# A vision block on one Trainium2 core: two of four adding tiles loaded whole and halved by GpSimd, the causal mask added by TensorE, the second variance moved to GpSimd

## What is computed

```python
def tok(x, channel_weights):                  # 14x14 patches of 16x16
    pooled = x.reshape(64, 12, 14, 16, 14, 16).sum(axis=(3, 5))
    return einsum('bcij,ce->bije', pooled, channel_weights).reshape(64, 196, 192)

def attn(x, ...):                             # 12 heads of 16
    q, k_, v = split(x @ Wqkv_w + Wqkv_b)
    scores = einsum('bthd,bshd->bhts', q, k_ / sqrt(16))
    scores = scores + triu(full(-10000.0), 1)              # causal mask
    attn_output = (softmax(scores) @ v) @ out_w + out_b
    selection = softmax((x @ sel_w + sel_b) / temperature)[..., 1:]
    idx = top_k(selection[..., 0], 14)                     # 14 of 196 tokens
    return x.at[idx].add((attn_output * selection)[idx])

def ffn(x, ...):
    return gelu(x @ in_weight.T + in_bias) @ out_weight    # 192 -> 768 -> 192

h = tok(x)
h = h + attn(layernorm(h))
h = h + ffn(layernorm(h))
```

## Time and profile before

| | |
|---|---|
| median of 3 runs | 710.67 us (710.17 to 711.61) |
| the profiled execution | 711.4 us, of which 709.7 us span |
| busy share of the span: TensorE, DVE, ScalarE, GpSimd | 82%, 75%, 48%, 22% |
| mean granted TensorE clock | 0.935 of 2.4 GHz |
| HBM read, written | 159.0 MB, 12.7 MB |
| mask adds of groups 0 and 15 start at | 108.1 and 671.4 us |

### The profile page before, as it was taken

One profiled execution on the slowest core, in us unless ns is written; L12 is line 12 of the kernel. 1 busy time (PEld: TensorE's weight loads), 2 busy tenths in 40 slices (PEclk: granted clock), 3 DMA queues, 4 the chain that ended last, 5 costly groups with the idle time before them and its releaser, 6 DMA issues.

```text
span 709.7 us, 12208 instructions
## 1 busy us (share of the span) xinstructions
PE 583.1 (82%) x3860; PEld 469.5 (66%) x3860; DVE 533.0 (75%) x1357; ACT 342.9 (48%) x826; POOL 156.6 (22%) x212
## 2 busy tenths in 40 slices
PE   0237268989997998989988959989998999899995
PEld 0126146667966786768776847768776877778774
DVE  0695968798979798888978865888989897855411
ACT  0000236565656556565656435565656474647451
POOL 1021312131232223222322203222322223102001
PEclk9967557999999999999999979999999999999999
DMA  9997998999999999999999998899999997501011
GB/s 315 298 330 221 289 308 201 304 270 316 259 315 267 317 253 313 286 296 277 282 316 251 286 231 248 229 304 241 305 308 278 280 282 214 109 9 37 4 35 40
DMA packets 66382, 172.56 MB, mean 243 GB/s; under 512 B 4457, under 2 KB 56873, under 8 KB 60171
## 3 DMA queue, kind: packets, MB, share of 16 engines
q1 hardware_dynamic: 32512, 110.11, 44.3%
q0 software_dynamic: 26112, 44.73, 35.5%
q10 hardware_dynamic: 7690, 16.89, 7.1%
...
## 4 chain that ended last, share of the span: by engine, by line
PE 32%; DVE 27%; DMA 18%; issue 13%; ACT 5%; POOL 2%; ACTq 2%; POOLq 0%; DVEq 0%
PE psO L590 9%; DVE R L888 8%; DMA X<-in_x 6%; DMA patch_sums<-R 5%; DMA OB<-in_ob 5%; PE psS L529 3%; PE psS L541 3%; PE psF L578 2%; PE psC L565 2%; DVE a_ln L898 2%; DVE y_ln L902 2%; DVE b_ln L900 2%; ACT Sm L703 2%; PE psS L550 2%; DVE mx L1014 2%
## 5 line engine op out<-in xcount | busy, mean ns | idle before, releaser
L590 PE MATMUL psO<-W,act 128*112 128x192 f32 x1344 | 268.2, 337 | 15.3 <-issue 8.6
L888 DVE TENSOR_REDUCE R<-X 128x42 f32<-128x1344 f32 (+1 forms) x112 | 235.7, 2138 | 29.6 <-DMA X<-in_x 29.5
L590 PEld LDWEIGHTS psO<-W,act 128*112 128x112 f32 x1344 | 220.8, 182 | 22.2 <-issue 9.9
L725 ACT ACTIVATE act<-psF 128x392 f32<-128x392 f32 x192 | 95.4, 497 | 131.8 <-PE psF L578 111.9
L344 POOL DMA_DIRECT2D X<-in_x x64 | 84.3, 1442 | 51.4 <-DMA X<-in_x 45.8
L578 PE MATMUL psF<-Stk,M1S 104*128 104x392 bf16 x192 | 66.9, 348 | 9.8 <-ACT act L725 9.3
L353 POOL TENSOR_TENSOR Pt<-Praw 48x196 f32<-48x196 f32 x16 | 8.5, 534 | 225.3 <-DMA Praw<-patch_sums 208.0
L703 ACT ACTIVATE Sm<-Sm,rinv 112x196 f32<-112x196 f32 x96 | 35.2, 445 | 21.7 <-DVE rinv L1019 21.5
L578 PEld LDWEIGHTS psF<-Stk,M1S 104*128 104x128 bf16 x192 | 18.8, 98 | 39.5 <-ACT act L725 24.0
L698 ACT ACTIVATE Sm<-Sm,nm 112x196 f32<-112x196 f32 x96 | 42.6, 445 | 4.8 <-issue 4.7
L732 ACT ACTIVATE obuf<-psO 112x192 f32<-112x192 f32 x112 | 36.0, 321 | 18.3 <-PE psO L594 18.3
...
(10 more groups left out here) (189 smaller groups left out, 870.6 us busy)
## 6 DMA issues: line engine op xcount, KB each, us to landing
...
X<-in_x POOLq DMA_DIRECT2D x64, 672.0 KB, 13.7
...
```

Source lines behind the costliest of these rows:

```text
L590: pe.matmul(to, act_sb[u % 2][:, m, i * OT:(i + 1) * OT], W2[:, m, :], start=(m == 0), stop=False)
L725: act.activation(act_sb[u % 2][:, n // 2, (n % 2) * (GT // 2):(n % 2 + 1) * (GT // 2)], psF[:, 0:GT // 2], ACT.Gelu).then_inc(act_F1.sem, 1)
L888: dve.tensor_reduce(R[:, r, t * TQ * N:(t + 1) * TQ * N].rearrange("p (q j) -> p q j", q=TQ), v, AX.XY, ALU.add).then_inc(dve_L, 1)
```

## The change

1. *Loads.* `ADDED` is now tiles 2 and 6. Tiles 0 and 4 (`HALVED`) are loaded whole by SyncE, and GpSimd adds their upper half rows to the lower ones in SBUF, one `tensor_tensor` of 128 x 1344 each. DVE sums 1344 values a partition of them as before. Tiles 1, 3 and 5 are summed whole, as before.
2. *Mask.* The left factor UB of the score matmul gets 56 more rows (partitions 64 to 119) with -10000 on a diagonal, the right factor FM gets 56 rows with 0 or 1 (position after the chosen token or not), so that the mask comes out of the same matmuls. DVE writes FM's rows instead of RM. Its add is gone; the maximum and the exponentials read the scores in PSUM.
3. *Second variance.* The four instructions and the root move from DVE to GpSimd. There the step that was one `scalar_tensor_tensor` is two instructions, so that the root has 14 and all of it 18.
4. *Plans.* The plans of GpSimd, TensorE, ScalarE and DVE are other strings; TensorE's and ScalarE's bodies also begin at another step than before. SyncE's is the same.

```diff
-ADDED = (0, 2, 4, 6)
-END = NG + 4
+ADDED = (2, 6)
+HALVED = (0, 4)
+END = NG + 5
@@ gpsimd
+            def halve(g, t):
+                pool.wait_ge(x_in[t], loaded(g))
+                v = X[t][:, :].rearrange("p (q r w) -> p q r w", q=TQ, r=QR)
+                pool.tensor_tensor(v[:, :, 0:2, :], v[:, :, 0:2, :], v[:, :, 2:4, :], ALU.add).then_inc(x_halved[t], 1)
...
+            def rsqrt(g, steps, t):
+
+                by_itself(pool)
+                pool.tensor_scalar(t["h"][:, :], t["x"][:, :], -0.5, None, ALU.mult).then_inc(steps.sem, 1)
+                pool.tensor_scalar(t["y"][:, :].bitcast(i32), t["x"][:, :].bitcast(i32), -0.5, float(0x5F3759DF),
+                                   ALU.mult, ALU.add).then_inc(steps.sem, 1)
+                for k in range(3):
+                    pool.wait_ge(steps.sem, steps.at(g, f"y{k - 1}" if k else "g"))
+                    pool.tensor_tensor(t["a"][:, :], t["y"][:, :], t["y"][:, :], ALU.mult).then_inc(steps.sem, 1)
...
+            def second_variance(g):
+
+                pool.wait_ge(dve_R1.sem, dve_R1.at(g, "y2"))
...
-            plan = ("X:4:1 X:6:1 K:v:2 K:d1:2 K:d2:2 X:0:0 c:s:4 X:2:0 P:s:1").split()
+            plan = ("c:s:5 H:0:1 H:4:1 P:s:2 X:6:1 A:var2:2 K:v:2 K:d1:2 K:d2:2 X:2:0").split()
@@ scalar
-                    act.activation(Sm[:, j, :], Sm[:, j, :], ACT.Exp, bias=nm[:, j:j + 1],
+                    act.activation(Sm[:, j, :], psS[0:ROWS, j // 2, (j % 2) * T:(j % 2 + 1) * T], ACT.Exp, bias=nm[:, j:j + 1],
-            plan = ("S:e2:2 S:e3:2 S:e4:2 S:e5:2 O:0:2 A:fm:1 S:n:2 A:e:1 O:1:2 K:H:1 S:t:2 K:M:1 K:L:1 K:k1:1 O:2:2 "
-                    "K:k2:1 R:st:0 f:0:1 O:3:2 f:1:1 f:2:1 O:4:2 f:3:1 f:4:1 R:ld:0 f:5:1 G:rs:1 f:6:1 O:5:2 C:XH:2 "
...
+            plan = ("S:e5:2 O:0:2 S:n:2 O:1:2 A:fm:1 A:e:1 K:H:1 S:t:2 O:2:2 K:M:1 K:L:1 K:k1:1 R:st:0 O:3:2 K:k2:1 "
+                    "f:0:1 f:1:1 f:2:1 O:4:2 f:3:1 f:4:1 R:ld:0 f:5:1 O:5:2 f:6:1 f:7:1 C:XH:2 G:rs:1 f:8:1 f:9:1 "
...
@@ vector
-                    dve.tensor_scalar(RM[:, :], kc("iota", ROWS), psS[0:ROWS, 0, ZR:ZR + 1], NEG, ALU.is_gt, ALU.mult).then_inc(dve_G.sem, 1)
+                    dve.tensor_scalar(FM[u % 2][ZR:KM, :], kc("iota")[ZR:KM, :], psS[ZR:KM, 0, ZR:ZR + 1], None, ALU.is_gt).then_inc(dve_G.sem, 1)
...
-                    dve.tensor_tensor(Sm[:, :, :].rearrange("p (k j) t -> p k j t", k=3),
-                                      psS[0:ROWS, :, 0:2 * T].rearrange("p k (j t) -> p k j t", j=2),
-                                      RM[:, :].unsqueeze(1).unsqueeze(1).broadcast_to([ROWS, 3, 2, T]), ALU.add).then_inc(dve_S.sem, 1)
...
-            plan = ("C:os:4 S:g:3 A:top:2 S:at:3 A:slots:2 G:ga:2 C:xh:3 L:0:0 G:u:2 L:1:0 S:sc:2 A:var:1 A:log:1 "
-                    "A:var2:1 S:ri:2 L:2:0 L:3:0 L:4:0 A:sel:1 L:5:0 L:6:0").split()
+            plan = ("C:os:4 A:sel:2 A:top:2 S:at:3 A:slots:2 G:ga:2 C:xh:3 L:0:0 G:u:2 L:1:0 S:sc:2 A:var:1 L:2:0 "
+                    "S:ri:2 A:log:1 L:3:0 L:4:0 L:5:0 L:6:0 S:g:2").split()
```

More of the change, by code:

```diff
@@ L32 @@
 ODD = 64
+KM = ZR + SLOTS
 PROWS = ODD + SLOTS
@@ L154, in program @@
         P = [sb(f"P{i}", [PF, T]) for i in range(2)]
-        FM = [sb(f"FM{i}", [ZR, T]) for i in range(2)]
+        FM = [sb(f"FM{i}", [KM, T]) for i in range(2)]
         prod = sb("prod", [HALF, 2, BC])
@@ L207, in program @@
         x_added = {k: sem(f"x_halves_added{k}") for k in ADDED}
+        x_halved = {k: sem(f"x_halved{k}") for k in HALVED}
         sums_out = [sem(f"sums_stored{k}") for k in range(2)]
```

90 lines of the change are left out of this document (57 added, 33 removed).

## The result

| | before | changed |
|---|---|---|
| median | 711.14 us (710.17 to 713.91, 4 runs) | 797.25 us (791.61 to 797.86, 4 runs) |
| ratio, 95% interval | | 1.118 (1.114 to 1.122) |
| profiled execution, its span | 711.4, 709.7 us | 797.4, 795.7 us |
| mean granted TensorE clock | 0.935 | 0.882 |
| start of the first and of the last of the 16 maxima | 109.5, 672.8 us | 118.9, 758.9 us |

The change makes the kernel 12% slower. The prediction was 704, its range 680 to 730.

A forecast was written before the change was run, and what follows sets the result against it. DVE's program was taken to keep TensorE waiting, by a little. 7.5 pairs from 73.7 to 72.9 us gave -6.0, edges -2.8, loop +2: -6.8 from 711.4, less 0.7 for the median, so 704, range 680 to 730.

The forecast's parts named there:

- What bounds the kernel: TensorE waits, by a little, for DVE's program; after the change TensorE bounds, pair 70.5 us without new waits, against 73.7.
- Mask: DVE's mask add of 1.37 us a group goes; maximum from PSUM stays 1.38, extra score matmul rows cost zero.
- Second variance: DVE loses 2.9 us a group; GpSimd gets 18 small steps at 0.24 each, 4.8 in all.
- rival 3: GpSimd's short chain is dear, deciding from about 0.3 us an instruction: 734 us, chance 0.09.
- The bound of 9: Upper bound in us for GpSimd's 18 second-variance steps, at 0.5 each.
- Loads: Halving adds of 2.84 us on GpSimd, DMA total from 79.8% to 70.9%; no direct gain, DVE waiting for no tile.
- The new wait: DVE instructions with two SBUF inputs blocked beside GpSimd's halving adds: 4.3 us a pair, net 2.4, bounds 0 and 11.4.
- rival 2: DVE held nearly through both halvings, gross 8.0 us a pair, net 6.1: 732 us, chance 0.18.
- a falling clock: Sign against the forecast: TensorE's clock falling for long after the new waits; no size given.
- The edges: Groups 0 and 15 each lose 1.4 us of mask add that nothing else covers: -2.8 us.
- The loop: At the engines' jump back in unrolled loops, TensorE's and ScalarE's stalls no longer coincide: +2 us, bounds 0 and +4.7.
- Rival 1: Halving adds fall beside DVE instructions that don't mind, pair 70.5 us: 686 us, chance 0.26.

The follow-up runs named there:

- the run with short halvings: The changed kernel with each halving add touching 48 values a partition instead of 1344, all else the same: 709.35 us, ratio 0.994.
- the good version: The changed kernel with halving adds moved apart, the second placed by group parity, loops unrolled, attention weights before tile refills: 669.4 us, ratio 0.938.
- the held kernel: The changed kernel itself, in which DVE instructions are held by GpSimd's halving adds: 797.25 us, ratio 1.118.
- the delay run: The good version plus one DVE instruction of about 2 us ahead of mask<-sl, only in groups where the chosen tokens' FFN ends: 715.4 to 738.4 us.
- the version with the halvings apart: The changed kernel, first halving add waiting for the top search's end, second moved behind tile 6's adding transfer: 726.0 us, ratio 1.016.

## Why the prediction was wrong

**What bounds the kernel**: right in the main. DVE's program was what TensorE waited for, though not at every place (the mask's add alone brought a quarter of its length); with 4.3 a group taken from it and nothing held, a pair falls to 69.9 at full clock and to 71.9 on the average of three (70.5 predicted).

**Mask.** The maximum out of PSUM 1.383 (1.38), the score matmuls with 56 more rows 0.343 (0.346 before, the first from the run with short halvings), both right where nothing is held. Worth 5 to 6 us by itself.

**Second variance.** 18 steps took 5.8 (249.10 to 254.90), not 4.8: 0.32 a step, over the 0.3 from which rival 3 was to decide. It didn't decide: with the halvings short and this chain in place the time was 709, and in the good version the move brings 57. The bound of 9 was not reached.

**Loads.** A halving add takes 3.24 on average, not 2.84 (3.0 where its record doesn't overlap the one ahead of it). DVE waits for no tile after the start, as forecast, and the DMA engines are relieved. But that it waited for none before either was a misreading: besides the 19.9 at the start there are six waits of 1.1 to 2.3 once a pair, 9.3 in all, each for tile 0's adding transfer, such as

```profile
212.88 1.55 DVE L888 TENSOR_REDUCE R<-X 128x42 f32<-128x1344 f32 x1 [2.24 <-DMA X<-in_x]
```

The changed kernel has none of them. I had put this gain at nothing; no run shows it by itself.

**The new wait: this step failed.** The mechanism was in the earlier trace rows; its size was wrong. I gave 4.3 a pair gross and 2.4 net. The holds are 9.9, and the pair grew by 15.6 over the average pair without them (17.6 over one at full clock). Three errors in it. First, I counted a hold as the rest of one halving; a waiting instruction is passed over until both in a row are done, when there is no gap between them. Second, I looked for two-input instructions only and put the second group's holds on scan and product; `mask<-sl`, one input, stands ahead of them and is held for nearly the whole. These two together are what rival 2 said, "held nearly through both halvings", with 8.0 gross; the trace had no row to tell it from the forecast. Third, I let a wait cost its own length. The clock added nearly as much again: 74.9 busy a pair instead of 66.0 to 67.3, in the held kernel, and 6.4 for 1.78 in the delay run. The prediction named a falling clock as what would make it wrong, and gave it no price, although has one: 37.02 busy at 0.89 against 34.41 at 1.00 for the same matmuls. The net also came from crediting 1.9 of waits as covered; whether they were, no run shows, and beside the clock it is small.

**The edges.** I gave -2.8; the first maximum came 9.5 later (whole tiles ahead of the last weights: with the weights first it is 12.7 earlier, in the version with the halvings apart), the end did not move. I had looked at what the first group no longer does, and not at the transfers that start with the kernel.

**The loop.** +2 was taken; with short halvings it is 22.0 against 10.8, +11.2, for the reason that I gave (the stalls no longer coincide), plus the clock after each and a stall of 5.0 at DVE's own jump, which the kernel before doesn't show and which I had not counted. In the changed kernel it is smaller: 52.44 + 42.56 = 95.0 against 87.5, 7.5.

**The rivals.** Rival 1 (686, harmless) is 709 with start and jump as they are, 23 above its number, of which 12.9 are the edges and 9.2 the loop. Rival 2 had the mechanism, and gave 732 because it lacked the clock. The upper end of the range was drawn from it, and so missed too.

Not settled: why the same wait of 1.78 brings the clock down in one window and not in another, and why the holds of the groups without the chosen tokens' FFN lower the clock less (0.92 against 0.81 to 0.85).
